# Moving two small operations from ScalarE to VectorE, and three steps to later places, in the software pipeline of a two-layer-model megakernel

## The chip, the cores and the metric

The kernel runs on one core of one Trainium2 chip. The metric is the device time of one execution in microseconds; 2821.27 us is the median of three runs before the change. All times below are microseconds unless marked ns. Engines are named as in the profile: PE is TensorE's matrix multiply, PEld its weight load, ACT is ScalarE, DVE is VectorE, POOL is GpSimd, SP is SyncE, which here only issues transfers.

## The reference, cut to what matters

The program computes a time-mixing layer, a small transformer with local attention (the part that the change touches), a full attention and a mixture of experts. The local transformer, six layers deep, on x of two sequences of 1024 tokens of 128 values:

```
def l2norm(t):
    return t / jnp.maximum(jnp.linalg.norm(t, axis=-1, keepdims=True), 1e-12)
...
def attn_layer(x, Wqkv, qs, ksc, Wo):
    qkv = x @ Wqkv
    q, k, v = jnp.split(qkv, 3, -1)          # 16 heads of 64
    q = l2norm(q) * qs
    k = l2norm(k) * ksc
    q = q * cos * scale + rotate_half(q) * sin * scale
    k = k * cos * inv + rotate_half(k) * sin * inv
    out = local_attention(q, k, v)           # windows of 32 tokens, each sees its own and the one before
    return out @ Wo
def ffn_layer(x, g, bln, W1, b1, W2, b2):
    mu = x.mean(-1, keepdims=True)
    var = ((x - mu) ** 2).mean(-1, keepdims=True)
    xn = (x - mu) / jnp.sqrt(var + 1e-05) * g + bln
    a, gate = jnp.split(xn @ W1 + b1, 2, -1)
    return a * jax.nn.gelu(gate, approximate=False) @ W2 + b2
for i in range(DEPTH):
    x = attn_layer(shift_tokens(x), ...) + x
    x = ffn_layer(shift_tokens(x), ...) + x
```

## The kernel before, in words

`local_transformer` treats the six layers as one stream of 96 slots (16 a layer); a slot is a block of 128 tokens of one of the two sequences. The attention part is done slot by slot, the feed-forward part on pairs of slots, called chunks (48 in all, 256 columns each). It is a software pipeline written out by hand: a loop over steps i from -4 to 100, in which each engine has a fixed list of functions, each for a slot or chunk at its own distance from i. `even(i, back)` gives the chunk at that distance, or nothing when the parity of i is the other one. So steps alternate. In an odd step PE does `variance`, and `up` (six matmuls in three blocks) of a chunk, and ACT does `inverse_dev`, `shift_norm` and `gate`, the last with two loads of activation tables; the text calls such a step heavy. An even step has `center`, `square`, `down` and `finish` and is called light. There are 48 heavy steps.

The chains that matter, for one slot g:

- PE projects q and k (`project_qk`, four blocks), ACT copies them out (`empty_qk`, line 956), squares them (`square_qk`, line 962), DVE sums the squares per head (`sum_squares`, line 1090), ACT inverts the norms (`invert_norms`: a Relu at line 971 that clamps from below, Ln at 973, Exp at 975), DVE scales (`normalise`, lines 1097 and 1104), POOL rotates (`rotate`, lines 728 and 733), PE transposes (`turn_qk`, line 805) and ACT copies the result out (`empty_turned`, line 996).
- PE computes the scores (`scores`, lines 820 and 826), DVE subtracts the row maximum (`shift_scores`, 1117 and 1119), ACT takes the exponent (`exponent`, 1013), PE transposes (`turn_prob`, 837), ACT copies out (`empty_prob`, 1002), PE multiplies by v (`weigh_v`, 855).
- For a chunk: PE subtracts the mean (`center`, 885), ACT squares (`square`, 1017), PE averages (`variance`, 890), ACT makes the inverse deviation (`inverse_dev`, 1021 and 1023), DVE scales (`norm`, 1154), ACT adds the bias vector (`shift_norm`, 1030), PE does `up` (899, 900), ACT `gate` (1040, 1042), DVE `hidden` (1160), PE `down` (908), DVE `finish` (1168).

Four PSUM banks (`TURN`) are handed round in the order of use on PE: a use waits (`wait_free`) until the bank of the fourth use before it has been emptied. So the third group of transposes of a step (`turn_qk` 1) waits for ACT's copy of the first, and the first two wait for `hidden` of the step before. The queues are in order, and every wait holds what stands behind it. In a heavy step ACT's list is: copies of turned q and k and of projections, `empty_att`, `inverse_dev`, `empty_v` 0, `empty_prob` twice, `shift_norm`, `square_qk`, `empty_v` 1, `exponent` twice, `gate`, `invert_norms`.

SP issues, per step, `load_x`, `look_back` (a copy of 32 columns of k within SBUF, line 638, which waits for `scores`), `load_v` (8 to 10 transfers of v, lines 619 to 633, the first behind a wait at line 615 for `weigh_v`), `load_f_x`, and weights of later layers. At the start, POOL clears buffers and sets the two columns of `least`; DVE makes its constants (`mask`, `ident_b`, `center_w`) as soon as the mask has come.

Of the kernel before, what the change touches and what calls it, by code (L numbers as in the profile page):

```python
# [9 lines left out]
ALU = mybir.AluOpType  # L10
# [3 lines left out]
P = 128  # L14
# [8 lines left out]
HEADS = 16  # L23
# [368 lines left out]
def local_transformer(nc, A, sb, sem, bank, ident, mean_w, eps, h_in, h_mid, padded):  # L392
# [7 lines left out]
    with ExitStack() as ctx:  # L400
        def buf(name, shape, dt=F32):
            return sb(f"lt_{name}", shape, dt, ctx=ctx)
# [17 lines left out]
        qk = buf("qk", [P, 2, 2 * INNER])  # L420
        ssq = buf("ssq", [P, 2, 2 * HEADS])
        rn = buf("rn", [P, 2, 2 * HEADS])
        least = buf("least", [P, 2])
        t_sin = buf("t_sin", [P, INNER])

        qr = buf("qr", [P, 2, 2 * INNER])
# [41 lines left out]
        def live(g):  # L468
            return 0 <= g < ALL
# [103 lines left out]
        with nc.Block(no_gpsimd_drain=True) as blk:  # L573
            @blk.sync
            def _(sp):
# [84 lines left out]
                for i in STEPS:  # L660
                    for layer in range(1, LAYERS):
                        for j, at in enumerate((-13, -12, -9, -7, -5, -3)):
                            if i == SLOTS * layer + at:
                                load_w(WCH * layer + j)
                    if even(i, -5) is not None and even(i, -5) >= 2:
                        load_x(even(i, -5))
                    if live(i + 2) and has_look(i + 2):
                        look_back(i + 2)
                    if live(i + 1):
                        load_v(i + 1)  # L670
                    if even(i, 3) is not None:
                        load_f_x(even(i, 3))

                    for layer in range(1, LAYERS):
                        n = i - (SLOTS * layer - 11)
                        if 0 <= n < 5:
                            load_scale(layer, n)
                        elif 5 <= n < 9:
                            load_layer(layer, n - 5)
# [13 lines left out]
            def _(pool):  # L693
# [58 lines left out]
                    pool.wait_ge(S.cleared, par + 1)  # L752
                    pool.memset(v[HD * par:HD * par + WIN, :, 0, :, :], 0.0).then_inc(S.cleared, 1)
                pool.wait_ge(S.cleared, 3)
                pool.memset(least[:, 0:1], -1e-24).then_inc(S.cleared, 1)
                pool.wait_ge(S.cleared, 4)
                pool.memset(least[:, 1:2], 1e-24).then_inc(S.cleared, 1)
                scale_tables(1)
                for i in STEPS:
                    late = [k for k in splits_at(i - 1) if k % WCH >= 4]  # L760
# [20 lines left out]
            def _(pe):  # L781
# [130 lines left out]
                for i in STEPS:  # L912
                    for j in range(4):
                        if live(i):
                            turn_qk(i, j)
                        if live(i + 2):
                            project_qk(i + 2, j)
                    if even(i, 5) is not None:
                        variance(even(i, 5))
                    if live(i - 2):  # L920
                        turn_att(i - 2, 0)
                        turn_att(i - 2, 1)
                    if live(i):
                        scores(i)
                    if live(i + 1):
                        project_v(i + 1, 0)
                    if even(i, 6) is not None:
                        down(even(i, 6))
                    if live(i - 1):
                        turn_prob(i - 1, 0)  # L930
                        turn_prob(i - 1, 1)
                    if live(i + 1):
                        project_v(i + 1, 1)
                    if live(i - 1):
                        weigh_v(i - 1)
                    if even(i, 4) is not None:
                        center(even(i, 4))
                    if even(i, 5) is not None:
                        for j in range(FB):
                            up(even(i, 5), j)  # L940
                    if live(i - 2):
                        project_out(i - 2)

            @blk.scalar
            def _(act):
# [16 lines left out]
                    act.activation(qr[:, g % 2, :], qk[:, g % 2, :], ACT.Square).then_inc(S.squared, 1)  # L962

                def invert_norms(g):

                    act.wait_ge(S.sumsq, g + 1)
                    if g == 0:
                        act.wait_ge(S.cleared, 5)
                    if g >= 2:
                        act.wait_ge(S.normed, g - 1)  # L970
                    act.activation(rn[:, g % 2, :], ssq[:, g % 2, :], ACT.Relu, bias=least[:, 0:1]).then_inc(S.clamped, 1)
                    act.wait_ge(S.clamped, g + 1)
                    act.activation(rn[:, g % 2, :], rn[:, g % 2, :], ACT.Ln, bias=least[:, 1:2]).then_inc(S.ln, 1)
                    act.wait_ge(S.ln, g + 1)
                    act.activation(rn[:, g % 2, :], rn[:, g % 2, :], ACT.Exp, scale=-0.5).then_inc(S.inv_norm, 1)  # L975

# [45 lines left out]
                    act.wait_ge(S.f_ln, c + 1)  # L1022
                    act.activation(f_rstd[:, :], f_rstd[:, :], ACT.Exp, scale=-0.5).then_inc(S.f_rstd, 1)

                def shift_norm(c):
                    layer = c // BLOCKS
                    if c % BLOCKS == 0:
                        wait_layer(act, layer)
                    act.wait_ge(S.f_scaled, c + 1)
                    act.activation(f_norm[:, :], f_norm[:, :], ACT.Identity, bias=lvec[:, layer % 2, 1:2])\  # L1030
                       .then_inc(S.f_normed, 1)

                def gate(c):
                    layer = c // BLOCKS
                    for j in range(FB):
                        n, m = FB * c + j, FROWS[j]
                        act.wait_ge(S.up, n + 1)
                        if c >= 1 and j == 0:
                            act.wait_ge(S.down, c)
                        act.activation(f_gate[0:m, j, :], bank[0:m, turn_bank("up", c, j), 0:PAIR], ACT.Gelu,  # L1040
                                       bias=lvec[0:m, layer % 2, 6 + j:7 + j]).then_inc(S.gated, 1)
                    act.preload_act_table_set("natural_log_exp_and_others")
# [4 lines left out]
                for i in STEPS:  # L1047
                    for j in range(4):
                        if live(i):
                            empty_turned(i, j)  # L1050
                        if live(i + 2):
                            empty_qk(i + 2, j)
                    if live(i - 2):
                        empty_att(i - 2, 0)
                        empty_att(i - 2, 1)
                    if even(i, 5) is not None:
                        inverse_dev(even(i, 5))
                    for k in splits_at(i):
                        if k % WCH < 4:
                            split_high(k)  # L1060
                    if live(i + 1):
                        empty_v(i + 1, 0)
                    if live(i - 1):
                        empty_prob(i - 1, 0)
                        empty_prob(i - 1, 1)
                    if even(i, 5) is not None:
                        shift_norm(even(i, 5))
                    if live(i + 2):
                        square_qk(i + 2)
                    if live(i + 1):  # L1070
                        empty_v(i + 1, 1)
                    if live(i):
                        exponent(i)
                    if even(i, 5) is not None:
                        gate(even(i, 5))
                    if live(i + 2):
                        invert_norms(i + 2)
                    if even(i, 4) is not None:
                        square(even(i, 4))
                    for k in splits_at(i):  # L1080
                        if k % WCH >= 4:
                            split_high(k)

            @blk.vector
            def _(dve):
                def sum_squares(g):
                    dve.wait_ge(S.squared, g + 1)
                    if g >= 2:
                        dve.wait_ge(S.clamped, g - 1)
                    dve.tensor_reduce(ssq[:, g % 2, :], qr[:, g % 2, :].rearrange("p (h d) -> p h d", d=HD), AX.X, ALU.add)\  # L1090
                       .then_inc(S.sumsq, 1)

                def normalise(g):
                    r = rn[:, g % 2, :]
# [52 lines left out]
                def norm(c):  # L1147
                    layer = c // BLOCKS
                    if c % BLOCKS == 0:
                        wait_layer(dve, layer)  # L1150
                    dve.wait_ge(S.f_rstd, c + 1)
                    if c >= 1:
                        dve.wait_ge(S.up, FB * c)
                    dve.scalar_tensor_tensor(out=f_norm[:, :], in0=bank[:, STAT, 0:PAIR], scalar=lvec[:, layer % 2, 0:1],
                                             in1=f_rstd[:, :], op0=ALU.mult, op1=ALU.mult).then_inc(S.f_scaled, 1)

                def hidden(c, j):
                    n, m = FB * c + j, FROWS[j]
# [5 lines left out]
                def finish(c):  # L1164
                    dve.wait_ge(S.down, c + 1)
                    if c % BLOCKS < BLOCKS - 1:
# [3 lines left out]
                                             scalar=lvec[:, c // BLOCKS % 2, 2:3], in1=block(h_mid, c),  # L1170
                                             op0=ALU.add, op1=ALU.add).then_inc(S.ff_out, 1)

                dve.wait_ge(S.mask, 16)
                for i in range(2):
                    dve.tensor_copy(mask[:, i, :].rearrange("p (a k) -> p a k", a=PAIRS),
# [918 lines left out]
```

## Time and profile before

| what | value |
|---|---|
| median of 3 runs | 2821.27 us (2820.28 to 2822.32) |
| the profiled execution's own time | 2821.27 us |
| its span, first to last instruction | 2819.3 us |
| PE busy | 2504.6 us, 89% |
| PEld busy | 2026.4 us, 72% |
| DVE busy | 2073.4 us, 74% |
| ACT busy | 1931.1 us, 68% |
| POOL busy | 1455.5 us, 52% |

The profiled execution took as long as the median; 1.97 us lie outside its span. The local transformer runs from about 111 to 1780 us. Busy shares are means over stages with different limits, and a PE that is busy is not PE at its peak, since the ends of matmuls are modelled; the start of one matmul to the start of the next tells more.

### The profile page before, as it was taken

Reading aid. Unit: us, or ns where it says so; the run is one execution under the profiler, and the core shown is the slowest. Engines: PE = TensorE matmul, PEld = TensorE weight load, DVE = VectorE, ACT = ScalarE, POOL = GpSimd, SP = SyncE. Lnnn points to the kernel's source line nnn. Section 1 sums busy time; section 2 is a strip of 40 time slices with the busy share of each in tenths; the row PEclk is TensorE's granted clock in tenths of the full one; section 3 lists DMA queues with packets and bytes.
Section 4 is the critical chain, followed back from the end, with each engine's and each line's share of the span. In section 5 each row is a group of like instructions: output and inputs, shape, how many; then the busy total and the mean of one; then the engine's idle time right before and its main releaser. Section 6 shows DMA issues by size and latency. Waiting matters only on the chain. (4 is left out here: it accounts for less than half of the span.)

```text
span 2819.3 us, 119352 instructions
## 1 busy us (share of the span) xinstructions
PE 2504.6 (89%) x52916; PEld 2026.4 (72%) x53012; DVE 2073.4 (74%) x2409; ACT 1931.1 (68%) x3809; POOL 1455.5 (52%) x1016
## 2 busy tenths in 40 slices
PE   4469999999999999999999998589999999986998
PEld 2157877777888788787878887366676676765887
DVE  5378888778888888887878885489888888973112
ACT  2367888788888888888888876566666666643443
POOL 0188887778788878877888774112122121211000
PEclk8689999999999999999999999799999999997999
DMA  0223433333333333333433332122223132210000
GB/s 33 61 68 91 98 95 83 83 94 84 95 92 96 83 94 88 100 79 91 98 88 77 90 77 53 44 48 59 61 47 71 38 70 59 47 34 16 16 22 30
DMA packets 274599, 193.96 MB, mean 69 GB/s; under 512 B 117545, under 2 KB 215857, under 8 KB 273969
## 3 DMA queue, kind: packets, MB, share of 16 engines
q1 hardware_dynamic: 274096, 186.49, 27.3%
q8 instruction: 410, 6.72, 1.0%
q14 instruction: 93, 0.75, 0.1%
HBM read 29.10 MB, written 1.05 MB: 11 GB/s over the span
## 5 line engine op out<-in xcount | busy, mean ns | idle before, releaser
L728 POOL TENSOR_TENSOR lt_t_sin<-lt_qk,lt_tab 128x512 f32<-128x512 f32 x384 | 685.6, 1807 | 263.1 <-DVE lt_qk L1097 260.6
L733 POOL TENSOR_TENSOR lt_qr<-lt_qr,lt_t_sin 128x1024 f32<-128x1024 f32 x192 | 455.5, 2372 | 27.9 <-POOL lt_t_sin L728 0.5
L1631 DVE TENSOR_REDUCE fa_neg_max<-bank 128x1 f32<-128x1024 f32 x256 | 301.2, 1218 | 91.2 <-PE bank L1458 90.9
L1090 DVE TENSOR_REDUCE lt_ssq<-lt_qr 128x32 f32<-128x2048 f32 x96 | 219.5, 2286 | 155.6 <-ACT lt_qr L962 155.6
L788 PE MATMUL bank<-lt_w_high,lt_x_high 128*128 128x512 f32 x576 | 281.2, 488 | 33.8 <-POOL lt_w_low L696 29.0
L1571 ACT ACTIVATE fa_prob<-bank,fa_neg_max 128x1024 f32<-128x1024 f32 x128 | 142.5, 1113 | 243.7 <-DVE fa_neg_max L1631 127.0
L1641 DVE STREAM_TRANSPOSE fa_prob_t<-fa_prob 128x1024 f32<-128x1024 f32 x256 | 301.8, 1218 | 0.0
L1481 PE MATMUL bank<-fa_prob_t,fa_v 32*64 32x128 f32 x16384 | 276.8, 274 | 23.7 <-issue 17.9
L1481 PEld LDWEIGHTS bank<-fa_prob_t,fa_v 32*64 32x64 f32 x16384 | 240.4, 130 | 71.5 <-issue 43.2
L805 PE MATMUL bank<-ident,lt_qr 128*128 128x128 f32 x1536 | 234.5, 276 | 32.3 <-POOL lt_qr L733 15.9
L1097 DVE TENSOR_TENSOR lt_qk<-lt_qk,lt_rn 128x2048 f32<-128x2048 f32 x96 | 233.0, 2427 | 31.9 <-ACT lt_rn L975 30.7
L1389 POOL TENSOR_TENSOR fa_qk_low<-fa_raw,fa_qk_high 128x256 fp32r<-128x256 f32 x128 | 90.0, 729 | 317.2 <-ACT fa_qk_high L1561 316.7
L805 PEld LDWEIGHTS bank<-ident,lt_qr 128*128 128x128 f32 x1536 | 184.1, 141 | 89.6 <-issue 36.5
L956 ACT COPY lt_qk<-bank 128x512 f32<-128x512 f32 x384 | 235.2, 614 | 10.0 <-POOL lt_t_sin L728 4.8
L1104 DVE TENSOR_TENSOR lt_qr<-lt_qk,lt_tab 128x2048 f32<-128x2048 f32 x96 | 231.1, 2408 | 3.3
L789 PE MATMUL bank<-lt_w_low,lt_x_high 128*128 128x512 f32 x576 | 229.7, 399 | 0.9 <-issue 0.9
L790 PE MATMUL bank<-lt_w_high,lt_x_low 128*128 128x512 f32 x576 | 229.9, 399 | 0.0
L981 ACT COPY lt_v_tok<-bank 128x512 f32<-128x512 f32 x192 | 112.7, 587 | 169.1 <-PE bank L790 169.1
L877 PEld LDWEIGHTS bank<-lt_prob_t,lt_w_o 128*128 128x128 f32 x1536 | 187.1, 192 | 9.8 <-issue 3.2
L855 PEld LDWEIGHTS bank<-lt_v,lt_prob_t 64*32 64x32 f32 x12288 | 129.6, 105 | 84.7 <-ACT lt_prob_t L1002 53.8
L877 PE MATMUL bank<-lt_prob_t,lt_w_o 128*128 128x128 f32 x1536 | 188.6, 275 | 2.0 <-issue 1.9
L962 ACT ACTIVATE lt_qr<-lt_qk 128x2048 f32<-128x2048 f32 x96 | 184.9, 1926 | 0.0
(226 smaller groups left out, 5707.1 us busy)
## 6 DMA issues: line engine op xcount, KB each, us to landing
lt_v<-lt_v_tok SPq DMA_DIRECT2D x576, 128.0 KB
fa_v<-fa_v_tok SPq DMA_DIRECT2D x256, 128.0 KB, 3.1
lt_v<-lt_v_tok SPq DMA_DIRECT2D x192, 64.0 KB
lt_k_t<-lt_k_t SPq DMA_DIRECT2D x84, 128.0 KB, 2.6
lt_v<-lt_v SPq DMA_DIRECT2D x168, 64.0 KB, 2.0
lt_w_raw<-in_lt_wqkv_dram SPq DMA_DIRECT2D x36, 256.0 KB, 3.8
lt_x_s<-h_in SPq DMA_DIRECT2D x96, 64.0 KB, 2.7
lt_f_x<-h_mid SPq DMA_DIRECT2D x96, 64.0 KB, 2.1
```

What stands on the lines that cost most here:

```text
L728: pool.tensor_tensor(dst[:, :, i, :], src[:, :, 1 - i, :], tab[:, g // 2 % 2, 1, at:at + 32].unsqueeze(1).to_broadcast([P, HEADS, 32]), AL ...
L733: pool.tensor_tensor(qr[:, g % 2, half], qr[:, g % 2, half], t_sin[:, :], ALU.add).then_inc(S.rotated, 1)
L788: pe.matmul(o, xh, w_high[:, k % WS, :], start=True, stop=False)
L790: return pe.matmul(o, xl, w_high[:, k % WS, :], start=False, stop=True)
L805: mm = pe.transpose(bank[:, turn_bank("turn", g, j), n * P:(n + 1) * P], qr[:, g % 2, (4 * j + n) * P:(4 * j + n + 1) * P], ident[:, :])
L877: mm = pe.matmul(o, w_o[:, layer % 2, hp, :], att_t[:, g % 2, hp, :], start=hp == 0, stop=hp == PAIRS - 1)
L956: act.copy(qk[:, g % 2, j * CH:(j + 1) * CH], bank[:, turn_bank("qk", g, j), :]).then_inc(S.proj_out, 1)
L1097: dve.tensor_tensor(heads, heads, r.unsqueeze(2).to_broadcast([P, 2 * HEADS, HD]), ALU.mult)\
L1104: dve.tensor_tensor(qr[:, g % 2, :].rearrange("p (a h d) -> p a h d", a=2, h=HEADS), qk[:, g % 2, :].rearrange("p (a h d) -> p a h d", a=2 ...
L1481: mm = pe.matmul(bank[d, 4 + a, 0:P].rearrange("p (u r) -> p u r", u=UPQ), v[rows, half % 2, kb, d], prob_t[rows, q % 2, par, :, 32 * kb:3 ...
L1631: dve.tensor_reduce(neg_max[:, u % 2, par:par + 1], bank[:, 2 * par:2 * par + 2, :].rearrange("p a n -> p (a n)"), AX.X, ALU.max, negate=T ...
L1641: dve.transpose(prob_t[:, q % 2, par, u % UPQ, :], prob[:, u % 2, par, :]).then_inc(S.turned, 1)
```

## The change

It does five things, all in `local_transformer`.

1. Clamping the sums of squares moves from ACT (Relu with a bias, 128x32, then Ln with a bias) to DVE (maximum with a constant tile of 1e-24, 128x32, behind a wait for DVE's own sum). It happens 96 times.
2. Adding the bias vector of the layer norm moves from ACT (`shift_norm`) to DVE (an addition of 128x256 with the vector broadcast, behind a wait for DVE's own product). It happens 48 times.
3. `variance` on PE moves from before `turn_att`, `scores` and `project_v` 0 to behind them, and `inverse_dev` on ACT to behind `empty_v` 0.
4. `look_back` moves behind `load_v` in SP's list.
5. POOL sets one tile `least` of 128x32 in place of two columns, and DVE waits for it (`cleared` at 4) ahead of its first constants.

```
-        least = buf("least", [P, 2])
+        least = buf("least", [P, 2 * HEADS])
...
+                    if live(i + 1):
+                        load_v(i + 1)
                     if live(i + 2) and has_look(i + 2):
                         look_back(i + 2)
-                    if live(i + 1):
-                        load_v(i + 1)
...
-                pool.memset(least[:, 0:1], -1e-24).then_inc(S.cleared, 1)
-                pool.wait_ge(S.cleared, 4)
-                pool.memset(least[:, 1:2], 1e-24).then_inc(S.cleared, 1)
+                pool.memset(least[:, :], 1e-24).then_inc(S.cleared, 1)
...
-                    if even(i, 5) is not None:
-                        variance(even(i, 5))
                     if live(i - 2):
                         turn_att(i - 2, 0)
                         turn_att(i - 2, 1)
...
                         project_v(i + 1, 0)
+                    if even(i, 5) is not None:
+                        variance(even(i, 5))
                     if even(i, 6) is not None:
                         down(even(i, 6))
...
-                    act.wait_ge(S.sumsq, g + 1)
-                    if g == 0:
-                        act.wait_ge(S.cleared, 5)
+                    act.wait_ge(S.clamped, g + 1)
...
-                    act.activation(rn[:, g % 2, :], ssq[:, g % 2, :], ACT.Relu, bias=least[:, 0:1]).then_inc(S.clamped, 1)
-                    act.wait_ge(S.clamped, g + 1)
-                    act.activation(rn[:, g % 2, :], rn[:, g % 2, :], ACT.Ln, bias=least[:, 1:2]).then_inc(S.ln, 1)
+                    act.activation(rn[:, g % 2, :], ssq[:, g % 2, :], ACT.Ln).then_inc(S.ln, 1)
...
-                def shift_norm(c):
...
-                    act.activation(f_norm[:, :], f_norm[:, :], ACT.Identity, bias=lvec[:, layer % 2, 1:2])\
-                       .then_inc(S.f_normed, 1)
...
-                    if even(i, 5) is not None:
-                        inverse_dev(even(i, 5))
                     for k in splits_at(i):
                         if k % WCH < 4:
                             split_high(k)
                     if live(i + 1):
                         empty_v(i + 1, 0)
+                    if even(i, 5) is not None:
+                        inverse_dev(even(i, 5))
                     if live(i - 1):
                         empty_prob(i - 1, 0)
                         empty_prob(i - 1, 1)
-                    if even(i, 5) is not None:
-                        shift_norm(even(i, 5))
...
+                    dve.wait_ge(S.sumsq, g + 1)
+                    dve.tensor_tensor(q, q, least[:, :], ALU.max).then_inc(S.clamped, 1)
...
+                    dve.wait_ge(S.f_scaled, c + 1)
+                    dve.tensor_tensor(f_norm[:, :], f_norm[:, :], lvec[:, layer % 2, 1:2].to_broadcast([P, PAIR]), ALU.add)\
+                       .then_inc(S.f_normed, 1)
...
+                dve.wait_ge(S.cleared, 4)
                 dve.wait_ge(S.mask, 16)
```

## Rows read from the trace of the kernel before

**Rows 1.** Windows view, one heavy step: us, then busy time and count of each engine

```profile
1007.52:1024.39 16.87, 16.16 (x336) 13.30 (x336) 13.28 (x16) 15.38 (x29) 12.90 (x10) 1.00 0.52 128
```

**Rows 2.** Timeline of that heavy step: start us, us, engine, line [idle before <-releaser]

```profile
1007.72 0.49 ACT L1021 ACTIVATE lt_f_squares<-bank,eps 128x256 f32<-128x256 f32 x1
1008.24 0.42 ACT L1023 ACTIVATE lt_f_squares<-lt_f_squares 128x256 f32<-128x256 f32 x1
...
1009.51 0.39 PE L790 MATMUL bank<-lt_w_high,lt_x_low 128*128 128x512 f32 x1
...
1009.99 0.58 ACT L981 COPY lt_v_tok<-bank 128x512 f32<-128x512 f32 x1 [1.34 <-PE bank L790]
1010.47 1.08 ACT L1002 COPY lt_prob_t<-bank 128x512 f32<-128x512 f32 x2
...
1011.43 0.53 ACT L1030 ACTIVATE lt_f_norm<-lt_f_norm,lt_lvec 128x256 f32<-128x256 f32 x1
1011.61 1.32 PEld L855 LDWEIGHTS bank<-lt_v,lt_prob_t 64*32 64x32 f32 x128 [0.58 <-ACT lt_prob_t L1002]
...
1011.84 1.92 ACT L962 ACTIVATE lt_qr<-lt_qk 128x2048 f32<-128x2048 f32 x1
...
1017.70 0.42 PEld L805 LDWEIGHTS bank<-ident,lt_qr 128*128 128x128 f32 x4 [0.23 <-issue]
...
1018.67 0.40 PE L790 MATMUL bank<-lt_w_high,lt_x_low 128*128 128x512 f32 x1
...
1018.91 0.60 PE L805 MATMUL bank<-ident,lt_qr 128*128 128x128 f32 x4
1019.10 0.32 ACT L971 ACTIVATE lt_rn<-lt_ssq,lt_least 128x32 f32<-128x32 f32 x1
...
1019.45 0.32 ACT L973 ACTIVATE lt_rn<-lt_rn,lt_least 128x32 f32<-128x32 f32 x1
...
1019.82 0.39 PE L790 MATMUL bank<-lt_w_high,lt_x_low 128*128 128x512 f32 x1
1019.94 0.57 ACT L996 COPY lt_q_t<-bank 128x512 f32<-128x512 f32 x1
...
1020.65 0.63 PE L805 MATMUL bank<-ident,lt_qr 128*128 128x128 f32 x4 [0.45 <-ACT lt_q_t L996]
```

**Rows 3.** Timeline of another heavy step, inside `weigh_v`

```profile
812.84 0.63 PE L855 MATMUL bank<-lt_v,lt_prob_t 64*32 64x64 f32 x37
...
813.98 1.12 PE L855 MATMUL bank<-lt_v,lt_prob_t 64*32 64x64 f32 x91 [0.52 <-issue]
```

**Rows 4.** Waits of PE, 120 to 1780 us: us in total, times, longest

```profile
PE bank L855 <- issue: 24.7, 28, 1.7
...
PE bank L805 <- ACT lt_q_t L996: 14.8, 29, 2.4
```

**Rows 5.** Instructions of single lines: ns min/median/max, first and last start

```profile
L971 ACT ACTIVATE lt_rn<-lt_ssq,lt_least x96: 321/322/324, 144.7 to 1715.0; 128x32 f32<-128x32 f32 x96
...
L1144 DVE TENSOR_TENSOR h_mid<-h_in,bank x96: 273/279/290, 205.3 to 1764.1; 128x128 f32<-128x128 f32 x96
```

**Rows 6.** Waits in SP's queue, 300 to 1700 us: us in total, times, longest

```profile
SPq L615 <- PE bank L855: 407.8, 84, 11.3
SPq L638 <- PE bank L826: 164.8, 60, 6.2
```

**Rows 7.** Timeline of the start of the local transformer

```profile
127.01 2.21 DVE L1175 CAST lt_mask<-lt_f_squares 128x512 bf16<-128x512 f32 x2 [16.97 <-DMA lt_f_squares<-in_mask_dram]
...
130.36 0.28 DVE L1178 TENSOR_TENSOR lt_center_w<-ident,mean_w 128x128 f32<-128x128 f32 x1
...
142.34 2.29 DVE L1090 TENSOR_REDUCE lt_ssq<-lt_qr 128x32 f32<-128x2048 f32 x1 [11.70 <-ACT lt_qr L962]
142.45 0.10 POOL L757 MEMSET lt_least<- 128x1 f32 x1
...
155.11 1.12 PE L805 MATMUL bank<-ident,lt_qr 128*128 128x128 f32 x4 [7.33 <-POOL lt_qr L733]
```

More of the change, by code:

```diff
@@ L1023, in inverse_dev, with gate @@
                     act.activation(f_rstd[:, :], f_rstd[:, :], ACT.Exp, scale=-0.5).then_inc(S.f_rstd, 1)
-                def shift_norm(c):
+                def gate(c):
                     layer = c // BLOCKS
@@ L1028, in shift_norm @@
                         wait_layer(act, layer)
-                    act.wait_ge(S.f_scaled, c + 1)
-                    act.activation(f_norm[:, :], f_norm[:, :], ACT.Identity, bias=lvec[:, layer % 2, 1:2])\
-                       .then_inc(S.f_normed, 1)
-                def gate(c):
-                    layer = c // BLOCKS
                     for j in range(FB):
@@ L1088, in sum_squares @@
                     if g >= 2:
-                        dve.wait_ge(S.clamped, g - 1)
-                    dve.tensor_reduce(ssq[:, g % 2, :], qr[:, g % 2, :].rearrange("p (h d) -> p h d", d=HD), AX.X, ALU.add)\
-                       .then_inc(S.sumsq, 1)
+                        dve.wait_ge(S.ln, g - 1)
+                    q = ssq[:, g % 2, :]
+                    dve.tensor_reduce(q, qr[:, g % 2, :].rearrange("p (h d) -> p h d", d=HD), AX.X, ALU.add).then_inc(S.sumsq, 1)
+                    dve.wait_ge(S.sumsq, g + 1)
+                    dve.tensor_tensor(q, q, least[:, :], ALU.max).then_inc(S.clamped, 1)
                 def normalise(g):
```

## The prediction, made before the changed kernel ran

> **What bounds the kernel now.** I read the page first: PE is busy in nearly every slice of the local transformer, and DVE, ACT and POOL each about 80% there, so shares alone do not name a bound. I then cut out one heavy step in the windows view [rows 1]: of 16.87 us PE is busy 16.16, ACT 15.38, DVE 13.28, POOL 12.90. PE and ACT both nearly fill it, so the question is which of the two ends it. The timeline answers [rows 2]. PE ends the last matmul of `project_v` 0 at 1009.90; ACT, idle for 1.34 until then, copies it at 1009.99, and from there to 1020.5 no ACT row of the step has an idle time in front of it: copies, `shift_norm`, squares, exponents, two table loads around the gate, the three norm operations, and at 1019.94 the copy of the first transposes of the next step. PE gets to that point early. Its third group of transposes needs the bank which that copy empties. Transposes start 0.24 after the third matmul ahead of them where nothing holds them (1018.67 to 1018.91), but here 0.83 (1019.82 to 1020.65): 0.59 lost. The first group also came 0.23 late (the weight load at 1017.70), for a bank that DVE's `hidden` had to leave, itself behind ACT's gate. So PE loses 0.59 + 0.23 = 0.82 at the seam of this heavy step, and ACT's chain from 1009.99 sets its end. The waits view counts 29 waits of this kind [rows 4].
>
> In other heavy steps PE is held up earlier: inside `weigh_v`, between two like matmuls with no semaphore between them, it stops for 0.52 [rows 3], and there are 28 such stops in all, 24.7 us, 0.88 each [rows 4]. Where the stop is longer than 0.82, PE is late itself and does not meet ACT's chain. So of 48 heavy steps a good half surely end with ACT; the others end with PE, some just.
>
> **The change part by part.** I take a heavy step with ACT as its end, in the times of [rows 2].
>
> *The Relu leaves ACT.* Its start to that of the Ln behind it is 1019.45 - 1019.10 = 0.35. It stands in the chain right ahead of the copy that PE waits for. The DVE sum that the Relu needed was there before (no idle time in front of it), and so will the maximum be. Gain on the chain: 0.35. In a light step it is gone too, but PE meets no ACT wait there; I count nothing.
>
> *The bias addition leaves ACT, the inverse deviation comes in.* `shift_norm` takes 1011.84 - 1011.43 = 0.41 of the chain, after the probability copies. `inverse_dev` stood before 1009.99, in ACT's 1.34 of idle time, free. Behind `empty_v` 0 it is no longer free: Ln to Exp 1008.24 - 1007.72 = 0.52, and the Exp to what follows some 0.31 (its 0.42 less the 0.11 by which the rows' other ops overlap: a copy lasts 0.58, the next starts 0.48 later). That is 0.83. Against that, PE reaches `project_v` 0 earlier, by the time of the variance that no longer stands ahead of it. Two matmuls of 256 columns; bounds from the rows: not under the 0.24 that a 512-column matmul takes to the next start, not over the 0.60 of four transposes; I take 0.43. So the copy of v starts at 1009.56, the Ln at 1010.04 (the variance, begun at 1009.31, is just done by then), the Exp at 1010.56, the probability copies at 1010.87 and 1011.35, and `square_qk` at 1011.83. Now it is 1011.84. The sum for the chain is 0.83 - 0.43 - 0.41 = -0.01: nothing, with 0.2 either way by those bounds.
>
> *What is late instead:* the probability copies start 0.40 later (1010.87 for 1010.47), and `weigh_v` waits for the second. Behind it in PE's queue stand `up`, `project_out` and the next step's transposes. PE's own path is 0.40 longer, with 0.82 of slack: it stays under ACT's, which ends at -0.35, since -0.82 + 0.40 = -0.42. The margin is only 0.07, so the gain is 0.35, and no more is to be had. In a step where PE stops inside `weigh_v`, the later start comes in front of the stop. If the stop is a late supply of instructions, its time does not depend on when `weigh_v` starts, and the variance, now behind the scores, also gives that supply 0.43 more. Then such a step ends 0.35 to 0.43 earlier as well. If the stop is a fixed length, the step pays up to 0.40. I take the first, since nothing but instructions can be missing between two matmuls of one group without a wait, and use 0.35 for all 48: 48 x 0.35 = 16.8 us.
>
> The Trainium skill bears on this in "Runtime: NRT & Kernel Launch", section on instruction fetch mechanics: the sequencer refills instructions in blocks of 256 while it runs, and crossing a block costs a mostly hidden bump. The trace disagrees on "hidden", with stops of 0.88 in the mean. By the page alone no step would stop, all 48 would gain 0.35, and the sum would be the same 16.8 without the doubt about the stopped ones.
>
> *DVE's new work.* Price of the maximum (128x32): under the 0.279 of a 128x128 addition [rows 5], over nothing; I take 0.2. The addition (128x256): over 0.279, and at most twice that; I take 0.42. DVE has 16.87 - 13.28 = 3.6 free in a heavy step [rows 1], so 0.62 fits if the places are right. The maximum stands behind the sum, ahead of `norm_att` 0, in front of which DVE soon waits for the gate anyway. In light steps it pushes `normalise` by 0.2; POOL follows. The addition has its input from the Exp at about 1011.0 and is done by 1012; `up` needs it only after `weigh_v`, which begins at 1011.61 now and later then. Cost: nothing; uncovered, 96 x 0.2 + 48 x 0.42 = 39 us.
>
> *SP's order.* `load_v` waits for `weigh_v` longer than `look_back` does for the scores [rows 6], so `look_back` is now issued at the end of the step, some 10 us later; its data are wanted in the step after next, most of a step away. `load_f_x` and `load_x` stand behind it and start one issue (0.6, my estimate from the spacing of other issues) later; both have more. No cost. Its many small packets leave the time just ahead of `weigh_v` and move to the start of the next step, ahead of `scores`; instruction supply may profit at one and suffer at the other. I count nothing.
>
> *The start.* DVE makes its constants from 127.01 to 130.64, 3.63 us, in a wait for the first squares. Now it must first wait for the tile `least`, which POOL sets at 142.4 [rows 7]; so the first `sum_squares`, at 142.34 now, starts at about 142.4 + 3.63 = 146.05, 3.7 later. ACT, DVE's normalise, POOL's rotation and PE's first transposes, for which PE sits idle 7.33, all hang on it. The exchange of Relu and maximum gives back 0.35 - 0.2. Cost, once: 3.6 us.
>
> *Sum.* The profiled execution took 2821.27, the same as the median. 2821.27 - 16.8 + 3.6 = 2808.1.
>
> **The rivals.**
> - *Only the ACT-ended steps gain.* The stopped steps end as now. About 24 x 0.35 = 8.4, less 3.6: 2816.5. For it: the 28 stops. Against: the stop would have to move with `weigh_v`. If they pay the 0.40 besides, 20 x 0.40 = 8 more: 2824.5.
> - *PE's path ends every step (the other side).* The later probability copies decide, if `weigh_v` slips by more than PE's slack of 0.82 less the 0.35 that ACT gives, 0.47. Price, if PE had no slack: 48 x 0.40 + 3.6 = 22.8, so 2844. For it: the margin is 0.07, and a variance that ends 0.2 later moves the Ln and all behind it. Against: a slip of 0.6 still costs only 0.13 a step, 2821 + 6 + 3.6 = 2831.
> - *DVE becomes the end.* All its additions on the path, and ACT's gain kept: 2821.3 + 39 - 16.8 + 3.6 = 2847. The rows speak against it (3.6 free). The Trainium skill, "VectorE: DVE Perf Modes", rules for kernel authors, says to minimise the number of chained DVE operations; the change adds 144. No row shows DVE short of time, so this has little chance.
> - *SP's order frees the instruction supply.* If half of the 24.7 us of stops goes in steps where PE ends: 12 us less, 2796 to 2798. If the stops ahead of the scores grow as much, nothing.
> - *The moves cancel and the steady state does not change* (the chain restarts later than I think): +3.6, 2825.
>
> **How the numbers follow.** The forecast has 0.50, with its own range 2803 to 2814 (0.25 to 0.43 a step). Only half the steps gain: 0.17. Cancelled: 0.06. PE's path ends: 0.10. DVE: 0.03. Freed supply on top: 0.14. A measurement tells 0.2%, 5.6 us, from no change. Faster, under 2815.6: 0.50 + 0.14 and a little of the half-gain case, 0.66. Same, up to 2826.9: 0.21. Slower: 0.13. The range 2796 to 2825 takes in the freed supply, the half gain and the cancelled case, and leaves out the two slow ones.
>
> **What would show it.** `weigh_v`'s idle time on ACT's copy grows from 0.58 to about 1.0 in heavy steps; the third transposes' wait falls from 0.59 to under 0.3; a pair of steps is 0.35 shorter; from the copy of v to `square_qk` it is 2.27, for 1.85 now; the first `sum_squares` starts near 146 and PE's first transposes near 158.7. The stops inside `weigh_v` become fewer or shorter in heavy steps. It is wrong if `up` waits for the addition, if `inverse_dev` starts later than 0.5 after the copy of v, or if the stops grow.

## The result, and the profile after

The changed kernel is slower: 2848.6 us in the median of 6 runs (2839.3 to 2852.6), against 2821.5 for the kernel before in the same job (6 runs). The ratio is 1.0097, with a 95% interval of 1.0081 to 1.0112. That is 27.1 us more, where 13 less were forecast. The profiled execution took 2849.61, its span is 2847.8. In the table of experiments further down the ratios leave out two far slower executions, one of 3426.4 us of the kernel before and one of 6640.9 us of clamp_alone, which the medians count.

First the profile's page: busy time, share of the span and count of instructions of each engine.

```profile
span 2847.8 us, 119442 instructions
PE 2514.4 (88%) x53012; PEld 2031.5 (71%) x53012; DVE 2183.9 (77%) x2553; ACT 1872.0 (66%) x3665; POOL 1468.1 (52%) x1015
```

ACT has 59 us less to do, as it should. DVE has 110 us more, and at their foretold prices the 144 new instructions come to 39. So some of them last far longer than thought. The view of single lines says which (ns min/median/max; times of the first and last start). The first row is the maximum, the second the bias addition:

```profile
L1078 DVE TENSOR_TENSOR lt_ssq<-lt_ssq,lt_least x96: 191/223/2353, 145.7 to 1742.5; 128x32 f32<-128x32 f32 x96
L1144 DVE TENSOR_TENSOR lt_f_norm<-lt_f_norm,lt_lvec x48: 424/1238/1986, 246.7 to 1801.0; 128x256 f32<-128x256 f32 x48
```

The shortest are as forecast, 0.19 and 0.42. The longest take 2.35 and 1.99. Below are the waits of PE, 120 to 1810 us (total, times, longest), to be held against [rows 4]:

```profile
PE bank L786 <- DVE h_mid L1131: 24.3, 28, 1.8
PE bank L853 <- ACT lt_prob_t L995: 24.1, 46, 1.1
PE bank L853 <- issue: 17.1, 24, 1.8
...
PE bank L803 <- ACT lt_q_t L989: 3.3, 4, 2.2
```

Line 803 is `turn_qk` (805 before): its wait for ACT, 14.8 us in 29 times in [rows 4], is nearly gone. The stops inside `weigh_v` (853, was 855) fell from 24.7 to 17.1, and stops of the same kind in `scores`, which [rows 4] leave out, grew from 12.1 (13 times) to 15.5 (14 times). Two waits are new or nearly so. `weigh_v` waits for the probability copies, 46 times 0.52 (before: 1.9 us in 3 times). And `project_qk` waits for DVE's residual addition (`h_mid`, line 1131), 28 times 0.87. The timeline of a light step shows where the second comes from (start, duration; in brackets the idle time ahead and its releaser):

```profile
841.99 2.29 DVE L1076 TENSOR_REDUCE lt_ssq<-lt_qr 128x32 f32<-128x2048 f32 x1 [1.60 <-ACT lt_qr L960]
...
843.26 2.37 POOL L733 TENSOR_TENSOR lt_qr<-lt_qr,lt_t_sin 128x1024 f32<-128x1024 f32 x1
...
844.31 1.37 DVE L1078 TENSOR_TENSOR lt_ssq<-lt_ssq,lt_least 128x32 f32<-128x32 f32 x1
...
845.61 0.68 DVE L1125 TENSOR_TENSOR lt_prob<-bank,lt_row_sum 128x512 f32<-128x512 f32 x1
...
845.72 0.23 ACT L966 ACTIVATE lt_rn<-lt_ssq 128x32 f32<-128x32 f32 x1 [2.24 <-DVE lt_ssq L1078]
...
846.21 0.27 DVE L1131 TENSOR_TENSOR h_mid<-h_in,bank 128x128 f32<-128x128 f32 x1
...
846.54 0.50 PE L786 MATMUL bank<-lt_w_high,lt_x_high 128*128 128x512 f32 x1 [0.87 <-DVE h_mid L1131]
```

Read it from the bottom. PE's second projection of the step needs the bank that the residual addition empties. That addition stands on DVE behind `norm_att` 0 (line 1125) and this behind the maximum. The maximum began at 844.31, when POOL was in the middle of its `rotate` addition, and ended at 845.68, 0.05 after POOL's at 845.63. With 0.19 in place of 1.37, all behind it would be 1.18 earlier, and PE's 0.87 would be gone. ACT's Ln, 2.24 idle, hangs on the same instruction; its waits for this sum grew from 45.3 us (51 times) before to 100.7 (51 times).

I call an instruction held when it has started but lasts until an instruction of POOL is over. Of all 96 maxima 44 started while POOL ran nothing and took 0.19. The other 52 started inside an instruction of POOL (their median is 1.08). In 4 of these POOL had at most 0.10 left, and they too took 0.19; the remaining 48 were held, for 0.25 to 2.35, and each ends 0.05 after POOL's. Of the 48 bias additions 44 were held, and they end 0.28 after POOL's.

The heavy step:

```profile
853.50 0.60 PE L888 MATMUL bank<-lt_f_squares,mean_w 128*128 128x256 f32 x2
853.75 0.59 ACT L974 COPY lt_v_tok<-bank 128x512 f32<-128x512 f32 x1 [2.38 <-PE bank L788]
853.94 1.03 PE L835 MATMUL bank<-ident,lt_prob 128*128 128x128 f32 x8
854.12 2.38 POOL L733 TENSOR_TENSOR lt_qr<-lt_qr,lt_t_sin 128x1024 f32<-128x1024 f32 x1
...
855.07 1.06 ACT L995 COPY lt_prob_t<-bank 128x512 f32<-128x512 f32 x2
...
855.72 1.07 DVE L1144 TENSOR_TENSOR lt_f_norm<-lt_f_norm,lt_lvec 128x256 f32<-128x256 f32 x1
...
856.02 1.92 ACT L960 ACTIVATE lt_qr<-lt_qk 128x2048 f32<-128x2048 f32 x1
856.18 1.29 PEld L853 LDWEIGHTS bank<-lt_v,lt_prob_t 64*32 64x32 f32 x125 [0.41 <-ACT lt_prob_t L995]
```

`variance` costs PE 853.94 - 853.50 = 0.44 (0.43 forecast). From the copy of v to `square_qk` it is 856.02 - 853.75 = 2.27 (2.27 forecast). The bias addition is held here too, until 856.79 with POOL's ending at 856.50, and nothing waits for it in this step.

To add it up I took, for 300 to 1700 us, the distance between the starts of neighbouring PE groups less the smallest distance at that place in the kernel before. In us, before and after:

| place | before | after |
|---|---|---|
| second projection of a light step, for the bank of the residual | 0 | 31.0 (30 times) |
| `weigh_v` of a heavy step, for the probability copies | 2.1 | 17.1 (40) |
| third transposes, for ACT's copy | 15.5 (27) | 2.7 |
| stops inside `weigh_v`, heavy steps | 22.8 (21) | 12.0 (13) |

The foretold gains are there, 12.8 and 10.8. The second line takes 15.0 of them back, and the first, foretold as nothing, costs 31.0. The sum of the four lines, 22.4, is most of the 26.5 by which the scores of slot 90 stand further from those of slot 10 (1356.8 for 1330.3 us). A pair of steps is thus 0.66 longer, where 0.35 shorter was forecast. (The last line depends somewhat on which steps are counted: with every heavy step of the window it is 25.8 before and 14.1 after.)

The start:

```profile
141.70 0.13 POOL L755 MEMSET lt_least<- 128x32 f32 x1
...
141.86 1.27 DVE L1166 CAST lt_mask<-lt_f_squares 128x512 bf16<-128x512 f32 x2 [32.16 <-POOL lt_least L755]
143.05 0.21 DVE L1168 CAST lt_ident_b<-ident 128x128 bf16<-128x128 f32 x1
...
143.39 2.27 DVE L1076 TENSOR_REDUCE lt_ssq<-lt_qr 128x32 f32<-128x2048 f32 x1
...
155.93 1.11 PE L803 MATMUL bank<-ident,lt_qr 128*128 128x128 f32 x4 [6.55 <-POOL lt_qr L733]
```

DVE waited as foretold, but its constants then took 1.53 us where [rows 7] have 3.63. The casts are shorter, 1.27 for 2.21. PE's first transposes come at 155.93 for 155.11: 0.8 us, not 3.6.

### The profile page after: what moved, and what is told of

Its sections match the earlier page's. It is cut to its first block and busy times, and to the rows that moved or that the text cites. A ratio compares the mean times of both kernels' runs of the same rounds, so it can differ in the third digit from the quotient of the medians.

```text
span 2847.8 us, 119442 instructions
## 1 busy us (share of the span) xinstructions
PE 2514.4 (88%) x53012; PEld 2031.5 (71%) x53012; DVE 2183.9 (77%) x2553; ACT 1872.0 (66%) x3665; POOL 1468.1 (52%) x1015
## 5 line engine op out<-in xcount | busy, mean ns | idle before, releaser
L1084 DVE TENSOR_TENSOR lt_qk<-lt_qk,lt_rn 128x2048 f32<-128x2048 f32 x96 | 225.2, 2346 | 13.4 <-ACT lt_rn L968 13.4
L853 PE MATMUL bank<-lt_v,lt_prob_t 64*32 64x64 f32 x12288 | 148.5, 225 | 45.4 <-ACT lt_prob_t L995 24.1
```

Source lines behind the costliest of these rows:

```text
L853: mm = pe.matmul(bank[WIN * w:WIN * w + WIN, value_bank(g, par), hp * HD:(hp + 1) * HD], prob_t[f, g % 2, hp, WIN * w:WIN * w + WIN], v[f, ...
```

## The experiments

Ratios are to the kernel before, run in the same job, with the 95% interval.

| kernel | ratio | interval | median us |
|---|---|---|---|
| undo_clamp | 1.0012 | 0.9995 to 1.0029 | 2828.5 |
| undo_bias | 1.0234 | 1.0217 to 1.0251 | 2894.1 |
| undo_order | 1.0050 | 1.0034 to 1.0066 | 2841.1 |
| undo_lookback | 1.0092 | 1.0074 to 1.0111 | 2854.1 |
| clamp_alone | 1.0094 | 1.0071 to 1.0118 | 2858.4 |
| pool_halves | 1.0035 | 1.0023 to 1.0047 | 2838.8 |
| one_input_max | 1.0092 | 1.0072 to 1.0113 | 2854.9 |
| bias_ln | 0.9906 | 0.9888 to 0.9924 | 2802.3 |
| order_alone | 1.0049 | 1.0030 to 1.0068 | 2838.7 |
| bias_alone | 0.9949 | 0.9931 to 0.9967 | 2814.6 |
| ln_only | 0.9956 | 0.9940 to 0.9972 | 2814.8 |
| bias_ln_order | 0.9963 | 0.9949 to 0.9977 | 2817.0 |

The first four ran in one job (kernel before: 2828.3), the next four in a second (2827.0), the last four in a third (2828.0).

### One part undone

**undo_clamp**, the changed kernel with the clamp back on ACT:

```
-                    dve.wait_ge(S.sumsq, g + 1)
-                    dve.tensor_tensor(q, q, least[:, :], ALU.max).then_inc(S.clamped, 1)
...
+                    act.activation(rn[:, g % 2, :], ssq[:, g % 2, :], ACT.Relu, bias=least[:, 0:1]).then_inc(S.clamped, 1)
+                    act.wait_ge(S.clamped, g + 1)
+                    act.activation(rn[:, g % 2, :], rn[:, g % 2, :], ACT.Ln, bias=least[:, 1:2]).then_inc(S.ln, 1)
```

> The changed kernel with the clamp alone put back on ACT (Relu, Ln with bias). Port theory (a DVE operation with two SBUF inputs waits for the POOL operation that is running, so the maximum holds DVE's queue, the residual addition comes late and PE's second projection of light steps waits for its bank, 31 us between 300 and 1700): those waits vanish, the Relu's 0.35 comes back on ACT's chain in some heavy steps (up to 10 us): 2817 to 2828. Rival, the reordering of variance and inverse_dev is what costs: stays at 2840 or more. Rival, SP's order: stays at 2840 or more.

1.0012: nearly all of the loss is gone. PE's waits, 300 to 1700 us:

```profile
PE bank L855 <- ACT lt_prob_t L1001: 21.3, 42, 0.5
...
PE bank L805 <- ACT lt_q_t L995: 11.5, 31, 0.9
PE bank L855 <- issue: 8.9, 17, 1.1
```

The wait for `h_mid` is not there. The wait of the transposes is back at 31 times, and that of `weigh_v` stays. So the maximum makes the wait for `h_mid`, and bias and order together do not shorten ACT's chain.

**undo_bias**, the changed kernel with `shift_norm` back on ACT behind `empty_prob`:

```
-                    dve.tensor_tensor(f_norm[:, :], f_norm[:, :], lvec[:, layer % 2, 1:2].to_broadcast([P, PAIR]), ALU.add)\
-                       .then_inc(S.f_normed, 1)
...
+                    if even(i, 5) is not None:
+                        shift_norm(even(i, 5))
```

> The changed kernel with the bias addition alone put back on ACT. Port theory: the addition lasts 1.22 in the mean (held by POOL) but stands in DVE's spare time of heavy steps, so DVE's relief brings little and ACT's heavy chain grows by 0.41: 2843 to 2862. Rival, the addition is the costly hold (48 times 0.8 us over its own length, 38 us): 2815 to 2825.

1.0234, 65.8 us above the kernel before: worse than anything expected. The maxima, PE's waits and a step's timeline:

```profile
L1088 DVE TENSOR_TENSOR lt_ssq<-lt_ssq,lt_least x96: 191/1689/2279, 144.8 to 1781.4; 128x32 f32<-128x32 f32 x96
```

```profile
PE bank L803 <- DVE lt_f_gate L1157: 43.4, 32, 1.9
PE bank L786 <- DVE h_mid L1141: 20.1, 21, 1.5
```

```profile
841.88 2.35 POOL L733 TENSOR_TENSOR lt_qr<-lt_qr,lt_t_sin 128x1024 f32<-128x1024 f32 x1
842.10 2.18 DVE L1088 TENSOR_TENSOR lt_ssq<-lt_ssq,lt_least 128x32 f32<-128x32 f32 x1
...
844.20 0.68 DVE L1135 TENSOR_TENSOR lt_prob<-bank,lt_row_sum 128x512 f32<-128x512 f32 x1
844.80 1.25 DVE L1157 SCALAR_TENSOR_TENSOR lt_f_gate<-bank,lt_lvec,lt_f_gate 128x256 f32<-128x256 f32 x3
...
845.42 0.63 PE L803 MATMUL bank<-ident,lt_qr 128*128 128x128 f32 x4 [1.00 <-DVE lt_f_gate L1157]
```

The maximum starts 0.22 after POOL and is held for all of it, to 844.28 with POOL's end at 844.23. Its median is 1.69 here, for 0.22 in the changed kernel: with the bias on ACT, DVE and POOL meet in the heavy steps too (near an `up`, which marks a heavy step, 44 of 45 maxima are held here and 6 of 45 in the changed kernel), and there `hidden`, which gives `turn_qk` its bank, is what comes late. The same instruction costs what its start relative to POOL's makes it cost. The size of that can't be read from a row in which the two meet otherwise.

**undo_order**, `variance` and `inverse_dev` back to their earlier places, and **undo_lookback**, `look_back` ahead of `load_v` again:

```
+                    if even(i, 5) is not None:
+                        variance(even(i, 5))
                     if live(i - 2):
                         turn_att(i - 2, 0)
```

```
+                    if live(i + 2) and has_look(i + 2):
+                        look_back(i + 2)
                     if live(i + 1):
                         load_v(i + 1)
-                    if live(i + 2) and has_look(i + 2):
-                        look_back(i + 2)
```

> The changed kernel with variance and inverse_dev alone at their old places. Port theory: the wait of weigh_v for the probability copies falls by 0.4 in 40 heavy steps (-15 us in the ledger), the stops inside weigh_v come back (+11 us), the DVE wait at the second projections stays: 2840 to 2852. Rival, the reordering is the cost: 2818 to 2828.

> The changed kernel with look_back alone ahead of load_v again. Port theory: nothing to tell, 2844 to 2853. Rival, SP's order is the cost (its small packets at the start of the step): 2820 to 2830.

The order costs 0.47% (1.0097 to 1.0050). Without it `weigh_v` no longer waits for ACT, but its stops are back at 18.7 us in 22 times:

```profile
PE bank L786 <- DVE h_mid L1131: 23.8, 27, 1.8
PE bank L853 <- issue: 18.7, 22, 2.2
```

The place of `look_back` makes no difference that these runs can tell.

### The maximum taken apart

**clamp_alone**, the kernel before with the clamp on DVE and the wait at the start:

```
-                    act.activation(rn[:, g % 2, :], ssq[:, g % 2, :], ACT.Relu, bias=least[:, 0:1]).then_inc(S.clamped, 1)
...
+                    act.activation(rn[:, g % 2, :], ssq[:, g % 2, :], ACT.Ln).then_inc(S.ln, 1)
...
+                    dve.wait_ge(S.sumsq, g + 1)
+                    dve.tensor_tensor(q, q, least[:, :], ALU.max).then_inc(S.clamped, 1)
```

> The kernel before with the clamp alone moved to DVE (and DVE's start behind the constant tile). Port theory: the maximum waits for POOL's addition of line 733 in light steps and, since DVE's other work is not shifted, perhaps in heavy steps too; PE waits for DVE at the second projection of light steps: slower by 20 to 65 us, 2842 to 2890. Rival, the price of the maximum is its own 0.19 and the slowness of the changed kernel comes from the parts together: 2815 to 2828.

1.0094: this part alone costs as much as the whole change.

```profile
PE bank L786 <- DVE h_mid L1140: 23.6, 22, 1.5
PE bank L853 <- issue: 15.9, 15, 1.9
PE bank L803 <- DVE lt_f_gate L1156: 13.2, 11, 1.9
```

**pool_halves**, the changed kernel with POOL's `rotate` addition cut from 128x1024 to two of 128x512. If the length of POOL's instruction sets the hold, the cut must shorten it, though POOL's work stays the same:

```
-                    pool.tensor_tensor(qr[:, g % 2, half], qr[:, g % 2, half], t_sin[:, :], ALU.add).then_inc(S.rotated, 1)
+                    for n in range(2):
+                        part = slice(INNER * a + CH * n, INNER * a + CH * (n + 1))
+                        pool.tensor_tensor(qr[:, g % 2, part], qr[:, g % 2, part], t_sin[:, CH * n:CH * (n + 1)], ALU.add)\
+                            .then_inc(S.rotated, 1)
...
```

The waits for `rotated` are renumbered to match.

> The changed kernel with POOL's addition of line 733 (128x1024, 2.37) cut into two of 128x512. Port theory: a held maximum waits for at most one half, so its longest time falls from 2.35 to about 1.4, PE's wait at the second projections from 31 to 5 to 15 us: 2822 to 2838. Rival, DVE is held by something else that lasts as long as the whole rotation: no change, 2845 to 2853.

```profile
L1081 DVE TENSOR_TENSOR lt_ssq<-lt_ssq,lt_least x96: 191/312/1324, 143.3 to 1725.4; 128x32 f32<-128x32 f32 x96
```

```profile
PE bank L856 <- ACT lt_prob_t L998: 20.6, 41, 0.5
...
PE bank L789 <- DVE h_mid L1134: 9.3, 17, 0.8
```

The longest maximum is 1.32 (was 2.35), the wait for `h_mid` 9.3 us (was 23.5 in this window), and 0.62% of 0.97% is won back. So the hold follows the length of POOL's instruction, and the time follows the hold, with DVE's code untouched.

**one_input_max**, the changed kernel with an immediate in place of the tile:

```
-                    dve.tensor_tensor(q, q, least[:, :], ALU.max).then_inc(S.clamped, 1)
+                    dve.tensor_scalar(q, q, 1e-24, None, ALU.max).then_inc(S.clamped, 1)
```

> The changed kernel with the maximum taken against an immediate, so DVE reads one SBUF tensor and no second. If the hold hangs on the second input alone, the maximum costs 0.1 to 0.2 each time and the time is that of the clamp undone or a little less, 2815 to 2828. If a one-input float32 operation of this kind takes the same port (the Trainium skill, SBUF - State Buffer, says so of the fast modes), it is held as before: 2843 to 2853.

```profile
L1078 DVE TENSOR_SCALAR lt_ssq<-lt_ssq x96: 181/436/2349, 143.9 to 1739.8; 128x32 f32<-128x32 f32 x96
```

It is held just as long (51 of 96 times), and the kernel stays at 1.0092. That the maximum has two inputs is not what matters here.

### The other parts alone

**bias_ln** is the kernel before with the bias addition on DVE, without the Relu, and with the Ln reading the sums directly. It clamps nothing: it takes ln(sum + 1e-24), where the other kernels clamp. **bias_ln_order** adds the moved `variance` and `inverse_dev` to it; **ln_only** leaves only the Relu out, with the same ln(sum + 1e-24); **bias_alone** and **order_alone** are the kernel before with that part.

```
-                    act.activation(rn[:, g % 2, :], ssq[:, g % 2, :], ACT.Relu, bias=least[:, 0:1]).then_inc(S.clamped, 1)
-                    act.wait_ge(S.clamped, g + 1)
-                    act.activation(rn[:, g % 2, :], rn[:, g % 2, :], ACT.Ln, bias=least[:, 1:2]).then_inc(S.ln, 1)
+                    act.activation(rn[:, g % 2, :], ssq[:, g % 2, :], ACT.Ln, bias=least[:, 1:2]).then_inc(S.ln, 1)
```

> The kernel before with the bias addition on DVE, and with the Relu left out: Ln of the sum plus 1e-24 in place of a clamp at 1e-24 (which differs from the reference only where a norm is next to nothing). variance, inverse_dev and look_back stay. Theory of ACT's chain: 0.41 and 0.35 leave the chain that ends heavy steps, weigh_v does not wait longer, no maximum on DVE: PE's wait at the third transposes of light steps (15.5 us) vanishes: 2800 to 2812. Rival, the held addition (1.2) makes DVE late in heavy steps: 2820 or more.

> The kernel before with the bias addition alone on DVE. ACT's chain loses 0.41 in heavy steps; PE's wait at the third transposes (15.5 us) falls to about 5: 2808 to 2817. If the held addition (1.2 to 1.5) makes DVE late: 2821 or more.

> The kernel before with the Relu alone left out (Ln of the sum plus 1e-24, no clamp). This is the term of the prediction by itself: 0.35 off ACT's chain where ACT ends the heavy step, 8 to 17 us: 2804 to 2815. If ACT's chain does not end the steps: 2819 to 2824.

> The kernel before with variance and inverse_dev alone moved. The prediction held that the move costs ACT's chain nothing net only together with the bias addition; alone it lengthens the chain by 0.4 a heavy step and delays weigh_v by 0.4: with the stops inside weigh_v as they are, 48 x 0.4 = 19, so 2838 to 2846; if the stops shrink as in the changed kernel (22.8 to 12.0 us), 2825 to 2837. If the move pays by itself: under 2818.

> The kernel of the bias addition on DVE without Relu, and with variance and inverse_dev moved as well. The move costs weigh_v's wait (15 us) and saves about 11 us of stops, as in the changed kernel: 2802 to 2818, not faster than without the move (2802). If the move pays once ACT's chain is short: under 2798.

bias_alone gains 0.51%, ln_only 0.44%, and together in bias_ln they gain 0.94%, nearly their sum. bias_ln beats both kernels of this study. bias_ln_order is the changed kernel without the maximum, its start and the new place of `look_back`: 0.9963 for 1.0097, so these three cost 1.34%, about 38 us, in the changed kernel's own order of work. In ln_only the wait of the third transposes for ACT falls to 1.3 us in 3 times, where the kernel before has 11.9 in 27 (both 300 to 1700 us). In bias_ln it is:

```profile
PE bank L855 <- issue: 20.5, 25, 1.8
...
PE bank L805 <- ACT lt_q_t L994: 1.4, 4, 0.5
```

And its bias addition is held as well, harmlessly:

```profile
L1147 DVE TENSOR_TENSOR lt_f_norm<-lt_f_norm,lt_lvec x48: 424/1486/2011, 244.1 to 1752.1; 128x256 f32<-128x256 f32 x48
```

order_alone costs 0.49%, and the step from bias_ln to bias_ln_order 0.57%, by the ratios. The waits of order_alone, 300 to 1700 us:

```profile
PE bank L855 <- ACT lt_prob_t L1002: 22.4, 43, 0.8
PE bank L805 <- ACT lt_q_t L996: 14.8, 31, 1.0
PE bank L855 <- issue: 12.6, 20, 1.3
```

## Why the prediction was wrong, point by point

The parts alone add up to the loss: clamp +0.94, order +0.49, bias -0.51, `look_back` +0.05 (from undo_lookback), together +0.97%, as measured. That the sum comes out so exactly is luck, because the parts are not independent: undone one at a time, clamp 0.85, order 0.47, bias -1.37 and `look_back` 0.05 add up to nothing. The clamp's own +0.94, less the Relu's -0.44 (ln_only), leaves +1.38 for the maximum and the start, about 39 us; bias_ln_order against the changed kernel gives 38.

- *The Relu leaves ACT, -16.8.* Right in kind. ln_only measures 2828.0 x 0.0044 = 12.4, and its interval (8 to 17) just takes in the 16.8. With bias and order moved as well (bias_ln_order) the gain is 0.37%, 10.5 us. So the account of ACT's chain holds, at a somewhat smaller size. (The forecast's own range, 2803 to 2814, is 2804 to 2813 by its own terms; nothing hangs on that.)
- *Bias out, inverse deviation in: nothing.* Right as a sum: -0.51% and +0.49% cancel. The chain was right to 0.01 (2.27 from the copy of v to `square_qk`, `variance` 0.44). Where bias_alone's 14.4 us come from is only partly seen. The third transposes' wait falls from 11.9 to 8.3. Over slots 10 to 90 PE's distances shrink by 4.4 us at the third transposes and by 4.2 at the first, which need the bank that `hidden` leaves, in profiled executions that differ by 6.6.
- *`weigh_v` later, absorbed by the slack.* Half right. The wait came, 40 times in the table above, and in the steps with a stop the stop shrank, by 10.8 us against the wait's 15.0. The sign that I named was wrong: not 1.0 idle for the weight load, but 0.41, because `variance` fills the rest, and a matmul wait of 0.52 in 46 steps, where the view of before has 3 such waits.
- *DVE's new work costs nothing.* **This step failed.** I priced the maximum at 0.2 from a 128x128 addition [rows 5], and that addition reads a PSUM bank and one SBUF buffer and is never held: its 273/279/290 ns was the wrong neighbour. Then I bounded the sum by DVE's free time in a heavy step [rows 1], while the damage is in light steps (42 of the 48 held maxima), where the maximum stands ahead of `norm_att` 0 and the residual addition, and PE's next projection waits for the latter. I named only `normalise` and POOL as what it pushes. In its place the runs show a hold to the end of POOL's instruction: 31.0 us of new waits in the changed kernel, 38 to 39 us by ratios.
- *`look_back`: nothing.* No difference to be told.
- *The start, 3.6.* 0.8. I carried 3.63 over from [rows 7]; the casts shrank from 2.21 to 1.27 and from 1.30 to 0.21 once they ran after POOL's clearing. The rows of before were held ones too: by their single instructions the two casts of `mask` end at 127.82 and 129.22, 0.29 and 0.28 after instructions of POOL that end at 127.53 and 128.94, and the cast of `ident_b` ends at 130.44, 0.09 after POOL's at 130.35.
- *Rival "DVE becomes the end", 2847.* Its number was met (2848.6) by luck, not by its working: it had every addition at its foretold price on the path, 39 us in all. What happened is that 48 of 96 maxima were held, while the bias additions, held too, cost nothing that the waits show. A chance of 0.03 was far too small for a step whose price none of the rows chosen showed.
- *Freed instruction supply.* The stops inside `weigh_v` do get fewer (22.8 to 12.0 us), but in trade for the wait ahead of them, and order_alone and undo_order show that this comes with the moved `variance` and `inverse_dev`, not with `look_back`. The stops in `scores` grew from 12.1 to 15.5.

The trace of the kernel before had such holds, and I did not look for them:

```profile
L728 POOL TENSOR_TENSOR lt_t_sin<-lt_qk,lt_tab x384: 1248/1281/3403, 148.0 to 1726.8; 128x512 f32<-128x512 f32 x192
L1104 DVE TENSOR_TENSOR lt_qr<-lt_qk,lt_tab x96: 2291/2293/3271, 148.0 to 1718.3; 128x2048 f32<-128x2048 f32 x96
```

Of POOL's 384 multiplications of line 728, 97 lasted over 1.4, and each of these started while one of DVE's multiplications of 128x2048 (lines 1097 and 1104, 192 in all) ran. Of these 192, 34 lasted longer than 2.31, and all 34 end 2.15 after an instruction of POOL. The residual addition, which reads a PSUM bank, never varies like that: 0.27 to 0.29 in all 96 rows.

The Trainium skill has the rule that I left out. "SBUF — State Buffer", section on the two separate sides of SBUF, says that DVE and GpSimd share a pair of ports under a lock held for a whole instruction: a DVE operation that uses both ports in its fast mode, or that has two inputs in SBUF while GpSimd reads SBUF, blocks fully against a GpSimd operation that started first. The trace agrees: held maxima end 0.05 after POOL's instruction, one-input ones 0.04 after (2.35 at the longest), while a DVE instruction that reads a bank and starts in the middle of a POOL instruction keeps its 0.69 us:

```profile
839.36 1.29 POOL L696 TENSOR_TENSOR lt_w_low<-lt_w_raw,lt_w_high 128x512 fp32r<-128x512 f32 x1
...
839.70 0.69 DVE L1106 TENSOR_TENSOR lt_prob<-bank,lt_row_max 128x512 f32<-128x512 f32 x1
```

By that rule, and this kernel's POOL rows of 2.37, each maximum would have had a range of 0.2 to about 2.5 us (an estimate).

## What to carry to other kernels

Before a small operation moves to DVE, ask whether it reads its tensors from SBUF alone (here the maxima, with one input or two, and the additions and multiplications with two were held), what POOL is running at that moment, and how long POOL's longest instruction is: here 0.19 us became up to 2.35. Price it by a row of the same kinds of operands, not only of the same size, and write down what stands behind it in the queue and who waits for that, in each kind of step. If such an operation can't be avoided, shorter instructions on POOL cut its price; if it can be dropped or folded into a neighbour (the Ln's own bias here), that is better than moving it.

## What the runs showed of the hardware that was not expected

- A held maximum of 128x32 ends 0.05 us after POOL's instruction, a held bias addition of 128x256 0.28 after it, a held multiplication of 128x2048 2.15 after it; alone they take 0.19, 0.42 and 2.29. In each case that is the instruction's own time less 0.14, so a hold costs what POOL has left at its start, less 0.14, and the 4 maxima that started with at most 0.10 left lost nothing.
- `sum_squares`, which reads SBUF too, was not held: 2.27 to 2.29 in all 96 rows of the changed kernel, also where it started inside an instruction of POOL, as at 841.99 above (POOL's runs from 840.60 to 843.12 in two parts).
- A maximum against an immediate is held like one against a tile (2349 and 2353 ns at the longest).
- Moving one ACT instruction of 0.41 changed the median duration of a DVE instruction elsewhere from 0.22 to 1.69 us, by shifting it against POOL, and the kernel's time by 1.37%.
